# Attention outputs brought into channel order by DMA instead of by transposes on TensorE

## Chip, cores and metric

The kernel runs on one core of a Trainium2 chip. The metric is the device time of one execution in microseconds (us), and the lower the better. A measurement of this kernel can tell a difference of about 0.2% from none.

## What is computed

A layer on x of shape (8, 1024, 256), float32: layer norm, then attention and a gated feed-forward part side by side, both added to x. The part that the change touches is the end of attention:

```python
q, k, v = heads(xn @ Wq + bq), heads(xn @ Wk + bk), heads(xn @ Wv + bv)   # 16 heads of 16
q, k = rotary(q), rotary(k)
att = (einsum('bhid,bhjd->bhij', q, k) + bias) / sqrt(16)                 # causal, T = 1024
att = softmax(where(causal, att, -inf))
y = einsum('bhij,bhjd->bhid', att, v)
y = y.transpose(0, 2, 1, 3).reshape(B, T, C)                              # channels: head * 16 + d
attention = y @ Wp + bp
```

The feed-forward part (16 columns of 64 neurons, of which a gate chooses one column for each token, with a layer norm behind it) is computed in the same loop and fills TensorE between the pieces of attention.

## The kernel before

The program is written by hand, engine by engine. One list of stages (function `iteration`) is walked by every engine, and each engine issues its own instructions of a stage; semaphores join them. So the order of the list is the order on every engine, the DMA queue of SyncE (SP) included. SP issues nearly all DMAs, one after another, and it waits in that order too.

The loop runs over 8 batches and in each over 4 groups of 4 heads: 32 iterations, called b0 g0 to b7 g3 below. An iteration holds 40 slots. A slot is one tile of transposed scores (keys on partitions, up to 512 queries in columns): TensorE multiplies (L1158), VectorE adds the near-diagonal bias where there is one (L1341, L1343, L1345), ScalarE takes the exponential (L1037) into `probs`. Every fourth slot TensorE multiplies `probs` by the values (`pv`, L1175) into `o_bank`, one PSUM bank: head h of the group stands in partitions 32h to 32h+15 as 16 values by 512 queries, and partition 32h+16 holds the softmax sum, since `v_aug` has a column of ones. The queries come in two halves. ScalarE copies `o_bank` to `o_sb` (stage `o_out`, L1045): half 0 after the pv of slot 16, half 1 in the closing part of the iteration.

Beside the slots stand, by the table `BESIDE`, the projection of a later chunk of x (`qk`, `v`), the rotary turn (GpSimd and VectorE), the split of q and k into three bf16 parts, the gate, the feed-forward part (`neurons` L1259, `columns` L1270), and `row` tiles: TensorE computes the next group's scores the other way round (L1196) and VectorE takes their maxima (L1365, L1370), from which comes the shift of the softmax. `with_rows` places these 40 tiles of an iteration by weights for TensorE and VectorE (`PE_TIME`, `DVE_TIME`).

At the end of an iteration (`CLOSING`): `load` (12 DMAs) and `load_v` fetch a later group's operands; `shift` reduces the maxima on VectorE; `shift_turn` transposes them on TensorE (L1243), ScalarE copies them (L1086), SP writes them by 3 DMAs into rows of `stack_q` (L812), and the first score of the next iteration waits for those DMAs. Between `shift_turn` and that score TensorE has the first 12 matmuls of `columns` (`OPENING`). VectorE's `center` (L1419) writes the normalized x of a later chunk.

How an output half gets to the result: `o_turn`, slot 21 for half 0, and just ahead of `shift_turn` for half 1: TensorE transposes `o_sb` in 4 pieces into one of the two PSUM banks of the pair (L1277); VectorE takes reciprocals of the sums (L1397) and multiplies (L1400) into `y`, with queries on partitions. In the last group of a batch and in g0 of the next, for each 256 tokens (chunks 0, 1 in g3; chunks 2, 3 in g0): `y_turn` transposes `y` back in 4 pieces (L1282, slots 26 and 32), ScalarE copies to `y_t` (L1100), and `project_begun`, `project` multiply by the output weights (L1288), VectorE adds the rest (L1533), SP stores (L827). The stages of `BANKED` take the two banks of the pair in turn, and the next user of a bank waits until the one before has been drained.

```python
elif stage == "o_turn":                                    # VectorE
    dve.wait_ge(bank_filled[i], use + 1)
    dve.reciprocal(inv[:, :, :], o4[:, :, :, D]).then_inc(inv_ready, 1)
    dve.wait_ge(inv_ready, k + 2)
    dve.tensor_tensor(dst..., o4[:, :, :, 0:D], inv..., ALU.mult).then_inc(bank_drained[i], 1)
```

## Time and profile before

| | |
|---|---|
| median of 3 runs | 1983.5 us (1981.84 to 1984.29) |
| the profiled execution | 1982.37 us |
| its span, first to last instruction | 1980.5 us |
| TensorE / VectorE / ScalarE / GpSimd busy | 91% / 82% / 56% / 32% |
| mean granted clock of TensorE | 0.978 of full |
| DMA | 189.44 MB, 96 GB/s on average |

PE is TensorE's matmul side, PEld its weight load, DVE is VectorE, ACT ScalarE, POOL GpSimd, SPq the DMA issues of SyncE. Times of rows are us from the start of the span. The chain is the sequence of work that ended last, followed back from the last instruction, so what lies on it costs time. The kernel is very regular: the transposes of half 0 come every 56.78 us in plain groups.

### The profile page before, as it was taken

What the parts mean: (1) busy time and instruction counts of PE and PEld (TensorE: products, weight loads), DVE (VectorE), ACT (ScalarE), POOL (GpSimd) and SP (SyncE); (2) the same over time, 40 slices, a digit from 0 to 9 for tenths busy, and PEclk for the clock granted to TensorE, in tenths of its full rate; (3) what the DMA queues carried; (4) which work ended last, traced back from release to release, by engine and by line L of the source; (5) the groups of instructions that cost most, each with busy time, mean ns of one, the idle gap of its engine ahead of it and who ended that gap; (6) DMA issues with size and microseconds to landing.
All of it is one profiled execution on the core that took longest, in us unless ns stands there. A gap on an engine that the chain in (4) does not pass through costs nothing.

```text
span 1980.5 us, 34962 instructions
## 1 busy us (share of the span) xinstructions
PE 1808.5 (91%) x10870; PEld 1041.2 (53%) x10870; DVE 1623.9 (82%) x5566; ACT 1112.3 (56%) x2150; POOL 629.2 (32%) x890
## 2 busy tenths in 40 slices
PE   5789999999999999999999999999999999999887
PEld 3555555554555555555555555565555555544433
DVE  5668988888888888888888888888888888878783
ACT  3326655556665566665555666555666555655544
POOL 6442333233333233233323333322323332311010
PEclk8789999999999999999999999999999999999998
DMA  6673223333233323422333332332333232232201
GB/s 188 191 163 97 78 88 99 104 94 96 91 92 100 113 68 97 123 88 86 98 96 90 112 92 76 103 109 78 102 97 105 84 100 83 65 87 70 59 12 49
DMA packets 220469, 189.44 MB, mean 96 GB/s; under 512 B 63387, under 2 KB 195371, under 8 KB 220284
## 3 DMA queue, kind: packets, MB, share of 16 engines
q1 hardware_dynamic: 219840, 186.83, 32.5%
q8 instruction: 87, 1.43, 0.3%
q14 instruction: 98, 0.80, 0.1%
q10 hardware_dynamic: 444, 0.38, 0.1%
HBM read 118.64 MB, written 69.27 MB: 95 GB/s over the span
## 4 chain that ended last, share of the span: by engine, by line
PE 52%; DVE 31%; ACT 7%; issue 6%; DMA 2%; SPq 1%; ACTq 0%; DVEq 0%; POOL 0%; POOLq 0%
PE rows L1196 10%; PE o_bank L1175 9%; PE scores L1259 9%; PE scores L1158 7%; DVE rows L1365 6%; DVE scores L1343 5%; DVE maxima L1370 5%; PE bank L1270 5%; PE bank L1288 3%; ACT probs L1037 3%; PE bank L1220 3%; PE scores L1261 2%; DVE maxima L1365 2%; PE bank L1214 2%; DVE scores L1345 1%
## 5 line engine op out<-in xcount | busy, mean ns | idle before, releaser
L1037 ACT ACTIVATE probs<-scores 128x512 f32<-128x512 f32 (+1 forms) x1280 | 672.0, 555 | 518.3 <-DVE scores L1343 302.9
L1370 DVE TENSOR_REDUCE maxima<-rows 128x1 f32<-128x512 f32 (+4 forms) x896 | 479.8, 552 | 167.2 <-PE rows L1196 163.5
L1158 PE MATMUL scores<-stack_q,stack_k 99*128 99x512 bf16 (+3 forms) x1536 | 431.8, 332 | 78.0 <-ACT probs L1037 70.0
L1196 PE MATMUL rows<-stack_k,stack_q 96*128 96x256 bf16 (+3 forms) x2048 | 460.9, 291 | 15.8 <-DVE maxima L1365 7.1
L1365 DVE CUSTOM_DVE_ANT_0 rows<-rows,near_rows 128x256 f32<-128x256 f32 (+1 forms) x1024 | 394.2, 431 | 48.0 <-PE rows L1196 47.4
L1196 PEld LDWEIGHTS rows<-stack_k,stack_q 96*128 96x128 bf16 x2048 | 175.2, 98 | 316.1 <-issue 114.4
L1343 DVE TENSOR_TENSOR scores<-scores,near_cols 128x256 f32<-128x256 f32 x768 | 321.1, 431 | 17.0 <-PE scores L1158 16.8
L1175 PE MATMUL o_bank<-probs,v_aug 128*32 128x512 f32 (+3 forms) x3072 | 317.1, 500 | 2.8 <-ACT probs L1037 2.8
L1259 PE MATMUL scores<-again,w_cols 128*128 128x256 f32 x1024 | 274.7, 391 | 3.1 <-DMA b_cols<-in_b_cols_dram 3.1
L1270 PE MATMUL bank<-w_proj,act_t 128*128 128x256 f32 x1024 | 255.4, 382 | 22.7 <-DVE y L1400 22.3
L1158 PEld LDWEIGHTS scores<-stack_q,stack_k 99*128 99x128 bf16 x1536 | 140.3, 98 | 250.1 <-ACT probs L1037 194.6
L1094 ACT ACTIVATE act_t<-scores,b_cols 128x256 f32<-128x256 f32 x256 | 107.5, 471 | 206.1 <-PE scores L1261 205.9
L1270 PEld LDWEIGHTS bank<-w_proj,act_t 128*128 128x128 f32 x1024 | 185.6, 189 | 53.5 <-DVE y L1400 30.7
L1259 PEld LDWEIGHTS scores<-again,w_cols 128*128 128x128 f32 x1024 | 183.7, 194 | 27.8 <-DMA b_cols<-in_b_cols_dram 3.2
L957 POOL TENSOR_TENSOR part<-qk,part 128x512 bf16<-128x512 f32 x64 | 74.1, 1158 | 271.3 <-ACT part L1078 271.2
L1365 DVE DVE_READ_ACCUMULATOR2_ANT maxima<- 128x1 f32 x1024 | 144.4, 141 | 0.1
L1220 PE MATMUL bank<-kept,w_qkv 128*128 128x256 f32 x496 | 134.6, 404 | 3.0 <-ACT kept L1050 3.0
L975 POOL TENSOR_SCALAR norm<-moments 128x2 f32<-128x2 f32 x32 | 7.3, 227 | 369.4 <-issue 369.0
L881 POOL TENSOR_SCALAR norm<-moments 128x2 f32<-128x2 f32 x32 | 7.2, 224 | 368.3 <-issue 362.2
L1175 PEld LDWEIGHTS o_bank<-probs,v_aug 128*32 128x32 f32 x3072 | 67.3, 108 | 91.4 <-issue 74.4
L1220 PEld LDWEIGHTS bank<-kept,w_qkv 128*128 128x128 f32 x496 | 95.0, 201 | 20.4 <-issue 7.1
L891 POOL TENSOR_TENSOR y2n<-y2n,gain 128x256 f32<-128x256 f32 x64 | 45.4, 731 | 141.4 <-DVE y2n L1526 141.4
(123 smaller groups left out, 2107.3 us busy)
## 6 DMA issues: line engine op xcount, KB each, us to landing
parts_d<-part SPq DMA_DIRECT2D x96, 256.0 KB, 2.2
stack_q<-parts_d SPq DMA_DIRECT2D x378, 64.0 KB, 3.0
stack_k<-parts_d SPq DMA_DIRECT2D x378, 64.0 KB, 2.3
kept_d<-kept SPq DMA_DIRECT2D x31, 512.0 KB, 2.9
again<-kept_d SPq DMA_DIRECT2D x31, 512.0 KB, 3.3
x<-in_x_dram SPq DMA_DIRECT2D x32, 256.0 KB, 3.4
turns<-turns_d SPq DMA_DIRECT2D x32, 256.0 KB, 2.9
v_d<-v SPq DMA_DIRECT2D x32, 256.0 KB, 2.4
```

Source lines behind the costliest of these rows:

```text
L957: pool.tensor_tensor(parts[2][:, KC * t:KC * t + KC, :], qk[:, t], parts[1][:, KC * t:KC * t + KC, :], ALU.subtract).then_inc(lo_ready, 1)
L1037: act.activation(probs[:, (g * NS + s) % PROBS, h, 0:width], ring[(rings + ring_n[1]) % RING][:, 0:width], ACT.Exp, scale=float(D) ** -0.5 ...
L1094: ins = act.activation(act_t[:, mm, :], ring[(rings + ring_n[1]) % RING][:, m * CH:(m + 1) * CH], ACT.Gelu, bias=b_cols[:, mm:mm + 1])
L1158: ins = pe.matmul(ring[(rings + ring_n[1]) % RING][:, c0:c0 + w], stack_k[g % 2][:, h, kb * P:(kb + 1) * P], stack_q[g % 2][:, h, q0:q0 + ...
L1175: ins = pe.matmul(o_bank[32 * h:32 * h + 32, HALF - w:HALF], v_aug[g % 2][:, kb, h, :], probs[:, (g * NS + s) % PROBS, h, c0:c0 + w], star ...
L1196: ins = pe.matmul(tile[:, c0:c0 + k1 - k0], stack_q[ag % 2][0:STACK, h, qb * P:(qb + 1) * P], stack_k[ag % 2][0:STACK, h, k0:k1], start=Tr ...
L1220: ins = pe.matmul(bank[:, half * CH:(half + 1) * CH], w_qkv[:, k, cols:cols + P], normed(g)[1][:, k, :], start=(k == 0), stop=(k == KC - 1))
L1259: pe.matmul(dst, w_cols[:, k, mm * P:(mm + 1) * P], ffn_t[:, k, :], start=(k == 0), stop=False)
L1270: ins = pe.matmul(bank[:, t * C:(t + 1) * C], act_t[:, m, t * P:(t + 1) * P], w_proj[:, m, :], start=(m == 0), stop=(m == EM - 1))
L1343: dve.tensor_tensor(tile[:, 0:2 * P], tile[:, 0:2 * P], near, ALU.add))
L1365: ins = dve.tensor_tensor_reduce(tile[:, c0:c0 + w], tile[:, c0:c0 + w], near_rows[:, ag * GH + h, 2 * P - w:2 * P], 1.0, LOWEST, ALU.add, ...
L1370: ins = dve.tensor_reduce(maxima[:, part, m:m + n], tile[:, c0:c0 + n * w].rearrange("p (n w) -> p n w", w=w), AX.X, ALU.max)
```

## The change

- The transposes of `o_sb` and of `y` on TensorE go, with their banks, VectorE's multiply and ScalarE's copy to `y_t`. `y_t` now holds 256 channels (2 times 128 partitions) by 1024 tokens.
- `o_move` (slot 17 for half 0; behind `o_out` 1 in the closing part): SP issues 4 DMAs that spread each head's row of sums over 32 partitions of 16 values (`sums`), and 4 that move each head's 16 rows of 512 into their channels of `y_t`.
- `o_recip` on VectorE (slot 22; half 1 in slot 2 of the next iteration), 128 by 16 from SBUF. `o_store` (23; 3): SP writes the reciprocals to DRAM. `o_fetch` (25; 6): SP waits for that DMA and reads them back, each head's row repeated over 16 partitions, into `inv_b` (64 partitions by 512).
- `o_scale` (28; 10) on GpSimd, in every second group: one multiply of 128 by 512, float32, in place in `y_t`, for two groups at once.
- `project_begun` waits for `o_scale`. Chunks 0 and 1 are projected in g3 from slots 30 and 34 (28 and 35 before), chunks 2 and 3 in g0 from slots 22 and 26.
- In g2, `load` and `load_v` go to the very end of the closing part. After the last group the chain `o_recip`, `o_store`, `o_fetch`, `o_scale` runs by itself ahead of the last two projections.
- `gate_th` and `ranked` share the memory of other small tiles.

```diff
-          21: [('gate', None), ('o_turn', 0)],
-          23: [('cast', 0)],
-          25: [('left', 0), ('middle', 0)],
-          26: [('y_turn', 0)],
-          28: [('load_k', None), ('project_begun', 0)],
+          17: [('hidden', None), ('o_move', 0)],
+          22: [('o_recip', 0)],
+          23: [('o_store', 0), ('cast', 0)],
+          25: [('left', 0), ('o_fetch', 0), ('middle', 0)],
+          26: [('rest_back', 0)],
+          28: [('load_k', None), ('o_scale', 0)],
+          30: [('cast', 1), ('project_begun', 0)],
+          31: [('left', 1), ('project', 0)],
+          34: [('middle', 1), ('project_begun', 1)],
+          36: [('project', 1)]}
+EARLIER = {22: [("project_begun", 2)], 23: [("project", 2)], 26: [("project_begun", 3)], 28: [("project", 3)]}
+for _at, _stage in ((2, "o_recip"), (3, "o_store"), (6, "o_fetch"), (10, "o_scale")):
+    BESIDE[_at] = BESIDE[_at] + [(_stage, 1)]
...
-CLOSING = [("load", None), ("load_v", None), ("neurons", (0, 0)), ("neurons", (0, 1)), ("pv", NS - 1), ("o_out", 1),
+CLOSING = [("load", None), ("load_v", None), ("neurons", (0, 0)), ("neurons", (0, 1)), ("pv", NS - 1), ("o_out", 1), ("o_move", 1),
...
-           ("neurons", (3, 1)), ("tie", None), ("o_turn", 1), ("shift_turn", None), ("center", None)]
+           ("neurons", (3, 1)), ("tie", None), ("shift_turn", None), ("center", None)]
...
+        late = [("load", None), ("load_v", None)] if g == NC - 2 else []
+        plan += [stage for stage in CLOSING if stage not in late] + late
...
+                    elif stage == "o_move":
+                        k, rows, dst = value_half(b, g, arg)
+                        sp.wait_ge(o_out, k + 2)
+                        wait(sp, inv_ready, k)
+                        for h in range(GH):
+                            sp.dma_start(sums[32 * h:32 * h + 32, :],
+                                         o_sb[32 * h + D:32 * h + D + 1, :].rearrange("o (n e) -> o n e", e=D)) \
+                                .then_inc(sums_in, 16)
+                        for h in range(GH):
+                            sp.dma_start(dst[h * D:(h + 1) * D], o_sb[32 * h:32 * h + D, :]).then_inc(y_in, 16)
+                    elif stage == "o_store":
+                        sp.wait_ge(inv_ready, k + 1)
+                        wait(sp, inv_in, k * 16)
+                        sp.dma_start(inv_d[k % 2].rearrange("h (n e) -> (h n) e", e=D), inv[:, :]).then_inc(inv_out, 16)
+                    elif stage == "o_fetch":
+                        sp.wait_ge(inv_out, (k + 1) * 16)
+                        wait(sp, y_ready, b * NG + (g // 2 * 2 + arg - 1))
+                        sp.dma_start(inv_b[rows, arg, :], bass.AP(inv_d.tensor, (k % 2) * GH * HALF,
+                                                             [[HALF, GH], [0, D], [1, HALF]])).then_inc(inv_in, 16)
...
+                    elif stage == "o_scale":
+                        if g % 2 == 0:
+                            continue
+                        pool.wait_ge(inv_in, (k + 1) * 16)
+                        pool.wait_ge(y_in, (k + 1) * GH * 16)
+                        dst = y_t[:, g % NG // 2, arg * HALF:(arg + 1) * HALF]
+                        pool.tensor_tensor(dst, dst, inv_b[:, arg, :], ALU.mult).then_inc(y_ready, 1)
...
-                        act.wait_ge(inv_ready, k + 1)
+                        wait(act, y_in, k * GH * 16)
+                        wait(act, sums_in, k * GH * 16)
                         act.activation(o_sb[:, :], o_bank[:, :], ACT.Copy).then_inc(o_out, 1)
...
                     elif stage in ("project_begun", "project"):
+                        pe.wait_ge(y_ready, projected(b, g) * NG + (NG - 1 + arg // 2))
```

## Rows read from the trace of the kernel before

**Rows 1.** The page, part 4: shares of the chain that ended last.

```profile
PE 52%; DVE 31%; ACT 7%; issue 6%; DMA 2%; SPq 1%; ACTq 0%; DVEq 0%; POOL 0%; POOLq 0%
```

**Rows 2.** Windows, slot 21 to shift, b0 g1, b0 g3: us, then busy PE, PEld, DVE, ACT, POOL.

```profile
232.52:260.48 27.96, 25.68 (x157) 11.76 (x155) 22.73 (x73) 17.61 (x37) 6.82 (x10) 1.00 0.32 90
...
346.03:377.16 31.13, 29.81 (x182) 16.01 (x180) 25.06 (x80) 18.26 (x39) 5.50 (x8) 1.00 0.43 120
```

**Rows 3.** Waits of TensorE, whole span: total us, times, longest.

```profile
PE bank L1270 <- DVE y L1400: 22.3, 30, 1.0
PE bank L1288 <- ACT y_t L1100: 11.5, 28, 0.8
PE scores L1158 <- DMA stack_q<-shift_t: 5.4, 8, 3.5
```

**Rows 4.** The chain in order of time, b3 g3: start us, us, what.

```profile
1047.31 0.48 PE bank L1277 x4
```

**Rows 5.** Timeline, end of b3 g2: start us, us, engine line, [idle before <- releaser].

```profile
1018.29 1.79 SPq L812 DMA_DIRECT2D stack_q<-shift_t  x3
1019.23 2.86 PE L1270 MATMUL bank<-w_proj,act_t 128*128 128x256 f32 x12 [0.97 <-DVE y L1400]
1021.92 0.38 PE L1158 MATMUL scores<-stack_q,stack_k 99*128 99x512 bf16 x1
1022.62 0.46 DVE L1343 TENSOR_TENSOR scores<-scores,near_cols 128x256 f32<-128x256 f32 x1
```

**Rows 6.** Timeline: load_v, shift ending b0 g1, b3 g3; shift, score ending b7 g2.

```profile
253.03 0.59 SPq L764 DMA_DIRECT2D v_in<-v_d  x1
260.22 1.79 SPq L812 DMA_DIRECT2D stack_q<-shift_t  x3
...
1073.55 0.59 SPq L764 DMA_DIRECT2D v_in<-v_d  x1
1078.56 1.79 SPq L812 DMA_DIRECT2D stack_q<-shift_t  x3
...
1930.29 1.77 SPq L812 DMA_DIRECT2D stack_q<-shift_t  x3
1933.48 1.44 PE L1158 MATMUL scores<-stack_q,stack_k 99*128 99x512 bf16 x3 [3.53 <-DMA stack_q<-shift_t]
```

**Rows 7.** One line each (durations ns min/median/max), and DMA issues (last: us to landing).

```profile
L812 SPq DMA_DIRECT2D stack_q<-shift_t x96: 508/591/1133, 147.0 to 1931.5; - x96
L702 SPq DMA_DIRECT2D stack_k<-parts_d x378: 302/426/1611, 66.9 to 1874.5; - x189
...
L1419 DVE TENSOR_SCALAR kept<-x,moments,rstd x62: 404/911/1431, 33.5 to 1664.3; 128x256 f32<-128x256 f32 x62
...
parts_d<-part SPq DMA_DIRECT2D x96, 256.0 KB, 2.2
...
v_in<-v_d SPq DMA_DIRECT2D x32, 256.0 KB, 3.1
...
stack_q<-shift_t SPq DMA_DIRECT2D x96, 8.0 KB, 1.8
```

**Rows 8.** Timeline, b3 g3: GpSimd's 128x512, the reciprocal, pv of slots 28 and 32.

```profile
1046.79 1.27 POOL L940 TENSOR_TENSOR qk<-qk,turns 128x512 f32<-128x512 f32 x1
...
1047.98 0.25 DVE L1397 RECIPROCAL inv<-bank 128x16 f32<-128x16 f32 x1
...
1051.44 1.07 PE L1175 MATMUL o_bank<-probs,v_aug 128*32 128x512 f32 x8
...
1056.66 1.07 PE L1175 MATMUL o_bank<-probs,v_aug 128*32 128x512 f32 x8
```

**Rows 9.** Timeline, the last 20 us: output copy and the last projections.

```profile
1965.12 0.60 ACT L1045 ACTIVATE o_sb<-o_bank 128x512 f32<-128x512 f32 x1 [0.98 <-PE o_bank L1175]
...
1968.85 3.43 PE L1288 MATMUL bank<-w_out,y_t 128*128 128x256 f32 x8 [0.84 <-ACT y_t L1100]
...
1973.55 1.97 PE L1288 MATMUL bank<-w_out,y_t 128*128 128x256 f32 x8 [0.84 <-ACT y_t L1100]
```

More of the change, by code:

```diff
@@ L208 @@
 NEEDS = {"qk_begun": "x_turn", "qk": "x_turn", "v": "x_turn", "hidden": "x_turn",
-         "project_begun": "y_turn", "project": "y_turn",
-         "y_turn": "o_turn", "y2_stats": "columns"}
+         "y2_stats": "columns"}
 class Order:
@@ L256, in iteration, with behind, here @@
                     plan.append(("o_out", 0))
-            plan += [(stage, arg + 2 * (g == 0) if stage in ("y_turn", "project_begun", "project") else arg)
-                     for stage, arg in BESIDE.get(i, [])]
+            plan += BESIDE.get(i, []) + EARLIER.get(i, [])
         plan += [("pv", s) for s in range((SLOTS - 1 - PV_AFTER) // GH + 1, NS - 1)]
-        plan += CLOSING
-        def here(stage):
-            return (has_front if stage in FRONT
+        late = [("load", None), ("load_v", None)] if g == NC - 2 else []
+        plan += [stage for stage in CLOSING if stage not in late] + late
+        def behind(stage, arg):
+            return stage in ("o_recip", "o_store", "o_fetch", "o_scale") and arg == 1
+        def here(stage, arg):
+            return (batch + g > 0 if behind(stage, arg)
+                    else g == NG - 1 if stage == "rest_back"
+                    else has_front if stage in FRONT
                     else batch + (g + LEAD + 1) // NC < B if stage in FRONT_AHEAD
@@ L268, in here @@
                     else has_load if stage in ("load_q", "load_k", "load", "load_v")
-                    else (g == NG - 1 or (g == 0 and batch > 0)) if stage in ("y_turn", "project_begun", "project")
+                    else (g == NG - 1 if arg < 2 else g == 0 and batch > 0) if stage in ("project_begun", "project")
                     else True)
-        plan = [(stage, arg) for stage, arg in plan if here(stage)]
+        plan = [(stage, arg) for stage, arg in plan if here(stage, arg)]
         if has_next:
@@ L274, in iteration @@
         for stage, arg in plan:
-            o.add(stage, g + (stage in FRONT_AHEAD) - (stage in FRONT_BEHIND), arg)
+            o.add(stage, g + (stage in FRONT_AHEAD) - (stage in FRONT_BEHIND) - behind(stage, arg), arg)
     if batch == B - 1:
+        for stage in ("o_recip", "o_store", "o_fetch", "o_scale"):
+            o.add(stage, NG - 1, 1)
         for k in range(NC // 2, NC):
-            o.add("y_turn", NG - 1, k)
             o.add("project_begun", NG - 1, k)
@@ L561, in ffn_of, with value_half @@
             return fb, c, fb * NC + c
+        def value_half(b, g, half):
+            rows = slice((g % 2) * GH * D, (g % 2 + 1) * GH * D)
+            return b * (2 * NG) + (2 * g + half), rows, y_t[rows, g % NG // 2, half * HALF:(half + 1) * HALF]
         def next_group(b, g):
@@ L1482, in body @@
                         step(5)
[L1483 removed]
+                        dve.tensor_reduce(first[:, :], tied[:, :, :], AX.X, ALU.max).then_inc(chosen, 1)
                         step(6)
[L1485 removed]
+                        dve.tensor_tensor(others[:, :, :], tied[:, :, :], each(first[:, :]), ALU.not_equal) \
                             .then_inc(chosen, 1)
```

85 lines of the change are left out of this document (30 added, 55 removed).

## The prediction

> **What bounds the kernel now.** I read the chain first: half of it is TensorE and a third VectorE [rows 1]. So neither engine's busy time can be taken as the time, and the next question is which of them holds which stretch. The chain in order of time repeats one pattern in every iteration. From `center` to about slot 15 it runs mainly over VectorE (row maxima, bias adds), from there to the shift mainly over TensorE, where a transpose of half 0 is on it with 0.48 us for four pieces [rows 4]. The windows show how tight TensorE is in the second part: busy 25.68 of 27.96 us in a plain group and 29.81 of 31.13 us in a group with two projections [rows 2]. From these two I take the rate at which TensorE work turns into time there: 3.17 us of span for 4.13 us of work, 0.77. The rest is hidden in waits on ScalarE and VectorE that become shorter.
>
> The waits say what the turns cost besides their own time: 22.3 us at the first `columns` matmul, which needs the bank that half 1's multiply has just drained, and 11.5 us in 28 waits of the projections for ScalarE's copy [rows 3].
>
> **Part by part.** The sum is made against the profiled execution, 1982.4 us (span 1980.5 and 1.9 around it), which is 1.1 below the median of the runs.
>
> *Half 0's turn goes.* TensorE loses 0.48 us [rows 4] in 31 iterations; the last is treated below. VectorE loses its multiply, while the reciprocal (0.25 us [rows 8]) stays, from SBUF. At 0.77 the 0.48 us are 0.37, times 31: -11.5 us. If TensorE counted in full, -14.9; if VectorE and ScalarE hid it all, 0.
>
> *The turns back go.* 28 of the 32 lie inside the loop ahead of the last group: 0.48 us for the same four pieces and 11.5 / 28 = 0.41 us of waiting [rows 3, 4]. At 0.77: 28 x 0.89 x 0.77 = -19.2 us; in full -24.9.
>
> *A new wait ahead of the projections in g3.* In g0 the operands of chunks 2 and 3 are scaled from slot 10 on, well ahead of slot 22. In g3 there are 8 slots between `o_recip` and `project_begun`. I place the chain in b3 g3. The reciprocal ends at 1048.2 [rows 8]. The store to DRAM: nearest row 2.2 us to landing [rows 7], so 1050.5. The fetch from DRAM, 128 KB: between 1.8 (the smallest row) and 3.1 (256 KB in pieces of 256 bytes) [rows 7]; I take 3.1, since a read behind a write had the longer rows, so 1053.6. GpSimd's 128 x 512 takes 1.27 us [rows 8]: about 1055.0 with its signals. TensorE gets there earlier than before. From the pv of slot 28 (1051.44) to that of slot 32 (1056.66) are 5.22 us [rows 8], of which 1.97 are a projection at full clock [rows 9] and 0.41 its wait; 2.8 us are left for four slots, so slot 30 comes 1.9 us behind 1051.44, and 0.96 us earlier for the two turns that are gone: 1052.4. TensorE stands still for 2.6 us, and queued behind it are the scores and rows that feed ScalarE and VectorE. Seven times 2.6 x 0.77: +14.0 us. The bounds: 1.3 us a time with a fetch of 1.8, +7; 5 us a time if both DMAs land over a microsecond later, +27.
>
> A rule of the Trainium skill speaks against this fetch: "DMA: Bandwidth & Descriptors", section "Why a DMA increments its semaphore by 16 and not by 1", says that a DMA is spread over the largest number of engines up to 16 that divides the slowest dimension of both sides. The fetch's source begins with a dimension of 4 heads, so 4 engines would carry it. No row here shows such a shape at this size. Were its landing 1 us longer by that, the stall would be 3.6 us and the forecast about 5 us higher.
>
> *The end of the iteration.* Here 0.48 us of turn and 0.74 us of wait (22.3 / 30) [rows 3, 4] leave TensorE, but something else is late next. `columns` could start 1.4 us ahead of 1019.23, and the score behind it can't follow: it needs the shift DMAs. These are issued from 1018.29 [rows 5], when ScalarE has come to its copy behind the last gelu, which the turn doesn't delay. Where only the DMAs hold the score it starts 3.19 us after the first issue (1930.29 to 1933.48) [rows 6]; that gives 1021.48 here instead of 1021.92 [rows 5]. VectorE is better off: without its reciprocal and multiply `center` starts some 0.6 us earlier, the row maxima follow, and the first bias add needs the score: 1021.48 + 0.38 + 0.07 = 1021.93 instead of 1022.62 [rows 5]. That is 0.69 us at the start of a stretch that VectorE holds, less 0.25 us for `o_recip` of half 1 in slot 2: 0.44 us. Eight iterations waited for the DMAs before [rows 3] and get nothing; 23 x 0.44 = -10.1 us. From above, all of 1.22 us counted 31 times: -38.
>
> This rests on SP. Between `load_v` and the shift DMAs it now has 8 issues and a wait for an output copy that is long done. An issue took 0.43 us (16 rows) or 0.59 us (the shift's) as a median [rows 7], so 3.4 to 4.7 us; the gap was 6.6 us in b0 g1 (253.62 to 260.22) and 4.4 us in b3 g3 [rows 6]. I take 0.5 us, 4.0 in all: hidden. If they don't fit, the excess is paid one for one. In g2 the loads are out of the way. They then start near 1020 in b3 and end their issue 6 to 7 us later; the late rows that need them come more than 12 us behind the shift, so I cost them at nothing. If that cover were gone, a microsecond would be paid 7 times. `o_store` and `o_fetch` of half 1 hold SP for some 2.5 us at slots 3 to 6, ahead of the DMAs of slot 7, which wait for ScalarE anyway.
>
> *The last group and the tail.* Nothing runs beside this chain at the end. `o_sb` is complete at 1965.72 [rows 9]. Four issues of 0.5 us, the last started 1.5 us in and landed after 1.8: 1969.1. Reciprocal 0.25; SP is through with 8 issues at 1969.8; store 2.2, fetch 3.1, multiply 1.27: 1976.4. The projection began at 1968.85 [rows 9], so +7.5 us. It ran at half clock then (3.43 against 1.97 us for 8), after TensorE had mostly waited; I assume the same again. Inside the last group the same stall of some 3 us is met by a stretch in which TensorE waits anyway, less the turns: +1.6. Together +9.1 us, between +5 and +14.
>
> **The sum.** -11.5 - 19.2 + 14.0 - 10.1 + 9.1 = -17.7 us. 1982.4 - 17.7 = 1964.7 in the profiled execution's terms, 1966 us as a median.
>
> **The rivals.** *B: TensorE is the bound and its time counts in full.* For it: busy 92% and more in the second half [rows 2]. Against it: the factor 0.77 and the shift DMAs. -14.9 - 24.9 - 38 + 7 + 9 = -62: 1922 us. Half way is as likely as the end, so I read this case as 1915 to 1952. Chance 0.22.
>
> *C: SP's queue takes the place of the turn, slower than before.* The 8 issues of half 1 stand straight ahead of the shift DMAs. It decides from 4.4 / 8 = 0.55 us per issue in g3 and 6.6 / 8 = 0.82 us in g1. The shift's own issues reached 1.13 us and the loads' 1.61 [rows 7], and a row of 64-byte pieces isn't in the trace. At 1.1 us they take 8.8 us: the first score is 2.2 us late after a gap of 6.6 and 4.4 us after one of 4.4. With about 16 and 7 such iterations +66 us; at 0.9 us, 16 x 0.6 + 7 x 2.8 = +29, and the 10.1 are lost: 1966 + 39 = 2005. Range 1985 to 2040, chance 0.15.
>
> *D: the new waits are near the upper bounds.* Stalls of 5 us in g3 (+27 in place of 14) and nothing at the iteration's end: 1966 + 13 + 10 = 1989; with one of the two, 1976 to 1979. Chance 0.12, and this is most of the case of no difference.
>
> *E: GpSimd's multiply holds up VectorE.* `center`'s instructions took 404 ns at least and 911 as a median, up to 1431 [rows 7], where they run beside GpSimd's work on `y2n`. There are 32 new multiplies of 1.27 us, next to maxima and bias adds. If each held VectorE for its length in half of the cases: 16 x 1.27 = +20, 1986 us. The 0.46 us bias adds show nothing of the kind. Chance 0.03. The Trainium skill, "SBUF — State Buffer", section "SBUF: two separate sides", says that the two engines share a port pair, locked for a whole instruction; by that rule an operation with one SBUF input and the other in PSUM isn't held, which keeps E small.
>
> **How the numbers follow.** The forecast A has 0.48, from 1953 to 1979 by the bounds of its terms. The range must reach into B below and into C and D above: 1935 to 1992 leaves out about half of B and most of C. Faster by over 0.2% (under 1979.5; 0.2% is about what a measurement tells from no change): A nearly whole, B, a third of D: 0.73. Within 0.2%: 0.08. Slower: C, half of D and E: 0.19.
>
> **What would show it.** The score that opens an iteration starts 3.2 us behind the first shift issue, and TensorE has an idle piece there that the shift DMAs end. The shift's issue follows ScalarE's copy without SP being late (C otherwise). The projections in g3 wait for GpSimd by 1 to 4 us, those in g0 don't. Plain groups get 0.8 us shorter (56.0 instead of 56.8), g0 some 2 us, g3 hardly at all. The tail from `o_sb` to the projection is near 10.5 us instead of 3. If plain groups shorten by over 1.5 us, B was right; if they lengthen, C.

## The result, and the profile after

The changed kernel takes 1999.55 us (median of six runs, 1993.13 to 2002.82) beside 1984.54 us of the kernel before in the same series: 1.0076 times, with a 95% interval of 1.0061 to 1.0092. It is slower by 15 us, where I had forecast 18 us faster (1966, range 1935 to 1992). The profiled execution has a span of 2001.0 us against 1980.5.

The page of the kernel after, parts 1 and 4; part 4 answers to [rows 1]. Its mean granted clock is 0.965 of full, where the kernel before had 0.978.

```profile
PE 1782.2 (89%) x10486; PEld 1001.3 (50%) x10486; DVE 1583.7 (79%) x5502; ACT 1093.3 (55%) x2086; POOL 670.2 (33%) x922
...
PE 49%; DVE 22%; ACT 8%; issue 6%; DMA 6%; SPq 4%; POOL 4%; ACTq 0%; POOLq 0%; DVEq 0%
```

GpSimd, SP's queue and the DMAs, together 3% of the chain before, hold 14% of it now. The waits of TensorE (total us, times, longest) answer to [rows 3]:

```profile
PE scores L1200 <- ACT probs L1085: 84.9, 145, 2.6
PE bank L1321 <- POOL y_t L992: 29.3, 9, 12.2
PE scores L1200 <- DMA stack_q<-shift_t: 20.1, 32, 5.5
PE bank L1312 <- ACT act_t L1143: 13.9, 31, 0.5
```

The two waits that the change was to take away, 22.3 and 11.5 us, are gone. In their place stand 29.3 us in nine waits for GpSimd's multiply (seven in g3 of b0 to b6, one in the last group, one in the tail), 14.7 us more for the shift DMAs and a new 13.9 for the gelu. The chain says the same: the kernel lost TensorE work and gained chains of small DMAs.

Where the time went, from one shift DMA to the next on SyncE's timeline (before and after; b0 g0 is the first iteration):

| stretch | before, us | after, us | difference | forecast |
|---|---|---|---|---|
| start to the first shift DMA | 147.0 | 148.5 | +1.5 | 0 |
| g0, g1 and g2 of b0 to b6 without b0 g0, 20 iterations | 1154.7 | 1140.3 | -14.5 | -23 |
| b0 g0 | 56.4 | 56.3 | -0.1 | -1 |
| g3 of b0 to b5, 6 iterations | 361.6 | 368.2 | +6.5 | 0 |
| b6 g3, b7 g0, g1, g2 (the work thins out) | 210.5 | 221.4 | +10.9 | -3 |
| last group and tail | 50.2 | 66.3 | +16.1 | +9 |
| sum | 1980.5 | 2001.0 | +20.5 | -18 |

The forecasts of the parts are my terms spread over the iterations that they were counted for. A plain group (g1 or g2) mostly took 56.78 us before; of the 14 in b0 to b6, 11 take 56.01 to 56.08 now, so the forecast of 56.0 holds. A g0 went from 59.90 us to between 58.4 and 58.6 (two at 59.2 and 59.4), where 57.7 was forecast. A g3, forecast level with before at 60.3, shows two kinds: 60.04, 60.27 and 60.28, or 62.23, 62.37 and 62.97.

The difference between the two kinds is seen in the timeline of b1 g3 of the kernel after, 584 to 592 us (start, duration, engine and line, idle time before and its releaser):

```profile
583.11 0.59 SPq L851 DMA_DIRECT2D inv_b<-inv_d  x1
587.20 1.26 POOL L992 TENSOR_TENSOR y_t<-y_t,inv_b 128x512 f32<-128x512 f32 x1 [1.21 <-DMA inv_b<-inv_d]
588.61 1.55 PE L1321 MATMUL bank<-w_out,y_t 128*128 128x256 f32 x4 [2.43 <-POOL y_t L992]
```

and in that of b0 g3, with the windows around it (us, busy PE, PEld, DVE, ACT, POOL, then the granted clock):

```profile
353.86 2.05 PE L1321 MATMUL bank<-w_out,y_t 128*128 128x256 f32 x4 [2.07 <-POOL y_t L992]
...
349.60:353.00 3.40, 2.19 (x13) 0.37 (x11) 2.49 (x7) 2.49 (x6) 2.13 (x3) 1.00 0.86 224
353.00:356.40 3.40, 2.54 (x7) 1.78 (x8) 0.03 (x1) 1.06 (x3) 0.71 (x1) 0.59 0.33 65
```

TensorE stood idle for 2.07 us, and behind that its clock was granted at 0.59 as a mean of the window, half level (1.2 GHz) for most of it: four projection matmuls took 2.05 us, which take 1.10 at the full level. VectorE did 0.03 us of work in 3.4 us, ScalarE a third of what it did before. In the kernel before nothing of the kind happens between 150 and 1736 us, and TensorE has no wait above 0.98 us there up to 1713. The first longer one stands in b6 g3, and the half level begins at 1736.3, right behind it:

```profile
1735.23 0.39 PE L1158 MATMUL scores<-stack_q,stack_k 99*128 99x512 bf16 x1 [1.83 <-ACT probs L1037]
```

In the kernel after, the half level begins at 353.6, 589.1, 1053.3 and 1408.3. The first three lie in g3, in exactly the three iterations of b0 to b5 that take 62 us or more. There the idle times were 2.07, 2.43 and 1.70 us; in those of 60.0 to 60.3 us they were 1.18, 1.04 and 1.18. The fourth lies in b5 g1, behind a wait of 1.21 us for ScalarE's probabilities, not for a projection.

The tail of the kernel after answers to [rows 9]:

```profile
1976.72 0.60 ACT L1094 ACTIVATE o_sb<-o_bank 128x512 f32<-128x512 f32 x1 [0.98 <-PE o_bank L1217]
1977.34 2.44 SPq L835 DMA_DIRECT2D sums<-o_sb  x4
1979.82 2.49 SPq L839 DMA_DIRECT2D y_t<-o_sb  x4
1980.93 0.25 DVE L1429 RECIPROCAL inv<-sums 128x16 f32<-128x16 f32 x1 [5.71 <-DMA sums<-o_sb]
1982.41 0.52 SPq L845 DMA_DIRECT2D inv_d<-inv  x1
1984.02 0.59 SPq L851 DMA_DIRECT2D inv_b<-inv_d  x1
1987.43 1.26 POOL L992 TENSOR_TENSOR y_t<-y_t,inv_b 128x512 f32<-128x512 f32 x1 [23.40 <-DMA inv_b<-inv_d]
1988.84 5.25 PE L1321 MATMUL bank<-w_out,y_t 128*128 128x256 f32 x16 [12.19 <-POOL y_t L992]
```

From `o_sb`'s end to the projection are 11.5 us where 3.13 stood before and 10.7 were forecast. Read it by its links: four issues of the sums 2.5, landing 1.1 behind the last, then the store could go at 1981.2 but SyncE is still issuing output moves until 1982.3; store 1.6, fetch 3.4, multiply 1.3, and 16 matmuls in 5.25 us at a mean granted clock of 0.70.

### The profile page after: what moved, and what is told of

It is laid out like the page before. It is cut to its first block, busy times and chain, and to the rows that moved or that the text cites. A ratio compares the mean times of both kernels' runs of the same rounds, so it can differ in the third digit from the quotient of the medians.

```text
span 2001.0 us, 34921 instructions
## 1 busy us (share of the span) xinstructions
PE 1782.2 (89%) x10486; PEld 1001.3 (50%) x10486; DVE 1583.7 (79%) x5502; ACT 1093.3 (55%) x2086; POOL 670.2 (33%) x922
## 4 chain that ended last, share of the span: by engine, by line
PE 49%; DVE 22%; ACT 8%; issue 6%; DMA 6%; SPq 4%; POOL 4%; ACTq 0%; POOLq 0%; DVEq 0%
PE scores L1301 11%; PE rows L1238 9%; PE o_bank L1217 8%; PE scores L1200 7%; DVE rows L1397 5%; DVE scores L1375 5%; PE bank L1312 4%; ACT probs L1085 4%; DVE maxima L1402 4%; DMA stack_q<-shift_t 3%; PE bank L1262 3%; PE scores L1303 3%; PE bank L1321 2%; SPq L827 2%; DVE maxima L1397 1%
## 5 line engine op out<-in xcount | busy, mean ns | idle before, releaser
L1200 PE MATMUL scores<-stack_q,stack_k 99*128 99x512 bf16 (+3 forms) x1536 | 437.9, 336 | 108.8 <-ACT probs L1085 84.9
L1312 PE MATMUL bank<-w_proj,act_t 128*128 128x256 f32 x1024 | 254.6, 381 | 13.9 <-ACT act_t L1143 13.9
L1005 POOL TENSOR_TENSOR part<-qk,part 128x512 bf16<-128x512 f32 x64 | 74.1, 1158 | 221.9 <-ACT part L1127 221.6
L1321 PE MATMUL bank<-w_out,y_t 128*128 128x256 f32 x256 | 74.0, 418 | 29.3 <-POOL y_t L992 29.3
```

What stands on the lines that cost most here:

```text
L1200: ins = pe.matmul(ring[(rings + ring_n[1]) % RING][:, c0:c0 + w], stack_k[g % 2][:, h, kb * P:(kb + 1) * P], stack_q[g % 2][:, h, q0:q0 + ...
L1312: ins = pe.matmul(bank[:, t * C:(t + 1) * C], act_t[:, m, t * P:(t + 1) * P], w_proj[:, m, :], start=(m == 0), stop=(m == EM - 1))
L1321: ins = pe.matmul(bank[:, t * C:(t + 1) * C], y_t[:, k, at:at + P], w_out[:, k, :], start=(k == 0), stop=(k == KC - 1))
```

## The experiments

All ratios are to the kernel before on the same chip in the same series. The theory from the two traces: the saved TensorE work is real, and what eats it is the idle time before the projection in g3, the fall of TensorE's clock that follows it, and the tail. The rivals: SyncE's queue, VectorE held by GpSimd's multiply, and the placing of the loads.

**Projections four to five slots later.**

```
-  30: [('cast', 1), ('project_begun', 0)],  31: [('left', 1), ('project', 0)],
-  34: [('middle', 1), ('project_begun', 1)],  36: [('project', 1)]
+  30: [('cast', 1)],  31: [('left', 1)],  34: [('middle', 1), ('project_begun', 0)],
+  35: [('project', 0)],  37: [('project_begun', 1)],  39: [('project', 1)]
```

> The changed kernel with only the projections of chunks 0 and 1 in g3 moved from slots 30/31 and 34/36 to 34/35 and 37/39. Theory S (the loss inside the loop is the stall of TensorE ahead of the first projection, 1.0 to 3.0 us in b0 to b6 and 4.5 us in the last group, and the stretches of half clock that follow it): the stalls vanish in b0 to b6, g3 takes 60.3 us or a little less in every batch instead of up to 62.97, and the whole goes from 1999.6 to about 1985 (7 x 1.8 x 0.77 = 10 for the stalls, 4 x 1.9 for the clock, less in part because the tail stays). Theory Q (SP's 10 DMAs more per half, or GpSimd's multiply beside VectorE, is what costs): the stall goes but the iterations keep their length, total within 3 us of 1999.6.

Measured: 1977.98 us, ratio 0.9977 (0.9958 to 0.9996), span 1973.5. The waits of TensorE:

```profile
PE scores L1202 <- ACT probs L1087: 88.8, 146, 2.2
...
PE bank L1323 <- POOL y_t L994: 14.0, 2, 12.4
```

Of the nine waits two are left, those of the last group and the tail. There is no half clock from 150 to 1713 us. Four slots turn the slower kernel into a slightly faster one: the wait was the cost, not the work that was added. The gain is 7 us more than expected, for the g3 are shorter than the 60.3 expected: of those of b0 to b5 three take 58.8 us, the others 60.2, 59.5 and 60.4. At the end of those three SyncE is late, by 0.7, 0.9 and 1.7 us: the shift is ready and its DMAs are not issued, which is rival C of the prediction. In b0 to b5 it shows only once the stall is gone. In b5 g3:

```profile
1524.65 0.27 ACT L1137 ACTIVATE shift_t<-bank 96x128 bf16<-96x128 bf16 x1
1526.61 1.85 SPq L829 DMA_DIRECT2D stack_q<-shift_t  x3
```

The issue comes 1.7 us behind the end of the copy, where it mostly is 0.02 to 0.03.

**TensorE kept at work in the wait.** Four matmuls of no use stand ahead of the wait of the first projection matmul (`arg` 0 in g3, `arg` 2 in g0). Each such float32 matmul stands as two in the trace.

```
+  if stage == "project_begun" and arg in (0, 2):
+      for _ in range(4):
+          pe.matmul(bank[:, 0:C], ident[:, :], w_out[:, 0, :], start=True, stop=True)
   pe.wait_ge(y_ready, ...)
```

> The changed kernel with four matmuls of 128x256 float32 (about 1.7 us of TensorE work whose result is overwritten) put ahead of the wait for GpSimd's multiply at the first projection of g3 and of g0. Theory S: what costs in g3 is the clock that falls behind the idle stretch more than the stretch itself. Then TensorE at work in place of waiting keeps full clock: no stretch at half clock in b0 to b5, g3 near 60.5 us in all of them (60.0 to 63.0 now), although work was added; g0 gets 1.3 us longer (7 x 1.3 = 9 us), so the total is about 1999.6 - 4 x 1.9 + 9 = 2001. If the clock falls for another reason, g3 keeps stretches of half clock and its 62 us in about four batches, and the total is 2008 or more.

Measured: 2001.14 us, ratio 1.0087 (1.0064 to 1.0109). The chain to the multiply is as long as before, so the projection starts no earlier; in b0 g3:

```profile
348.53 1.89 PE L1319 MATMUL bank<-w_out,ident 128*128 128x256 f32 x8
350.29 1.13 PE L1324 MATMUL bank<-w_out,y_t 128*128 128x256 f32 x4
...
346.00:350.00 4.00, 3.64 (x20) 1.90 (x21) 3.17 (x8) 3.06 (x7) 3.38 (x4) 1.00 0.83 213
350.00:354.00 4.00, 4.00 (x24) 2.11 (x23) 2.32 (x8) 1.53 (x3) 0.24 (x1) 1.00 0.28 48
```

The clock stays at the full level and the projection at 1.13 us. The g3 of b0 to b5 take 60.5 to 61.3 us, none 62 or more. What is won there is paid again in g0, where there was no wait to fill: 60.1 to 61.7 us in place of 58.4 to 59.4. The total is the 2001 that was expected, but it is made of a gain and a loss; the groups say more. In g3 the clock follows TensorE's idle time, and without its fall the three g3 of 62 us or more are 1.7 to 2.2 us shorter, though the wait is as long. One stretch at half level is left in b0 to b5, against the expectation: at 475.0 in b1 g1 (58.9 us), behind a wait of 1.69 us for ScalarE's probabilities, which these matmuls don't touch.

**The fetch in four DMAs.**

```
-  sp.dma_start(inv_b[rows, arg, :], bass.AP(inv_d.tensor, (k % 2) * GH * HALF, [[HALF, GH], [0, D], [1, HALF]]))
+  for h in range(GH):
+      sp.dma_start(inv_b[first_row:first_row + D, arg, :],
+                   bass.AP(inv_d.tensor, ((k % 2) * GH + h) * HALF, [[0, D], [1, HALF]]))
```

> The changed kernel, but each fetch of the inverse sums is four DMAs of 16 partitions in place of one DMA of 64. In the changed kernel GpSimd's multiply begins 4.0 us after the fetch's one issue in g3, where I had taken 3.1 from the landing of v_in. Theory F: the one DMA is slow in itself (its 64 rows go through few of the core's DMA engines); then each of the four lands faster, the fourth issue is only 1.8 us after the first, and from the first issue to the multiply it is again 4 us or a little less: the stalls before the projection in g3 stay at 1 to 3 us (mean 1.8), and the time stays within 3 us of the changed kernel's (ratio to the kernel before 1.006 to 1.009). Theory L: the landing is a fixed delay of the write and the semaphore, whatever the DMA's shape; then the fourth lands 4.0 us after its own issue, 5.8 after the first, the stalls grow by 1.8 us each, clock falls become more frequent, and the time is 12 to 20 us above the changed kernel's (ratio 1.014 to 1.018). In the tail F gives about the same 12.2 us of idle time, L gives 14. [...]

Measured: 1985.17 us, ratio 1.0013 (1.0001 to 1.0025); the profiled span is 1982.3. Both theories missed the total. The links in b1 g3, which answer to the rows of 583.11 to 588.61 above:

```profile
576.77 1.72 SPq L853 DMA_DIRECT2D inv_b<-inv_d  x4
579.95 1.26 POOL L995 TENSOR_TENSOR y_t<-y_t,inv_b 128x512 f32<-128x512 f32 x1 [0.39 <-DMA inv_b<-inv_d]
581.36 1.10 PE L1324 MATMUL bank<-w_out,y_t 128*128 128x256 f32 x4 [1.39 <-POOL y_t L995]
```

From the first issue to the multiply are 3.18 us here, 4.09 with one DMA. Wherever GpSimd waited for the fetch in g3 or g1, it was 3.1 to 3.4 us with four and 3.7 to 5.1 with one (3.4 only in the tail). The DMA table has 1.8 us from issue to landing for each of the four. So theory F was right that the one DMA is slow in itself, and too cautious in its size: splitting wins about 0.9 us although three issues come on top. The sentence of the Trainium skill weighed in the prediction ("DMA: Bandwidth & Descriptors", section "Why a DMA increments its semaphore by 16 and not by 1") fits these times: by it the one DMA, whose source begins with four heads, goes through 4 engines and each of the four, whose first dimension is 16, through 16. Which engines carried them isn't read from a row here.

The nine waits fell from 29.3 to 24.5 us in total, and that was worth 12 to 15 us. A part of the difference is the clock. In b0 g3 the stall fell from 2.07 to 1.19 us and the projection's four matmuls from 2.05 to 1.10:

```profile
349.21 1.10 PE L1324 MATMUL bank<-w_out,y_t 128*128 128x256 f32 x4 [1.19 <-POOL y_t L995]
```

All stalls of b0 to b5 lie at 0.87 to 1.50 us now, and behind none of them does the clock fall; the six g3 take 59.9 to 60.5 us. Of the 18.7 us between the two spans 3.8 lie ahead of the end of b0 g0, where the kernels hardly differ; that leaves 15. The medians differ by 14.4, and the ratios by 0.0063, which is 12.5 us. By stretches, the six g3 are 7.1 us shorter, for waits that are 2.7 us shorter; the last group and tail 0.9; and 5.5 lie in the light iterations, where a part may be chance, as is told below.

The waits are not shorter by 0.9 us each, for the fetch is not always the last link. In b0 to b5 GpSimd waited for it in three g3 of the kernel after (1.12, 1.21 and 0.47 us), and in one here (0.39). In the others the multiply stands right behind GpSimd's own split of q and k, which in the kernel after (L1005) had waited for ScalarE each time. In b5 g3 of that kernel:

```profile
1515.25 1.16 POOL L1005 TENSOR_TENSOR part<-qk,part 128x512 bf16<-128x512 f32 x1 [1.29 <-ACT part L1127]
1516.36 1.26 POOL L992 TENSOR_TENSOR y_t<-y_t,inv_b 128x512 f32<-128x512 f32 x1
```

There a quicker chain of DMAs brings nothing more; the multiply ahead of the split was not tried.

**GpSimd's multiply left out.** The division of the outputs by the softmax sums is not computed.

```
-  pool.tensor_tensor(dst, dst, inv_b[:, arg, :], ALU.mult).then_inc(y_ready, 1)
+  pool.sem_inc(y_ready, 1)
```

> The changed kernel with GpSimd's multiply left out (its waits stay, its semaphore is raised at once); left out of the computation is the division of the outputs by the softmax sums. Theory S (the multiply is one link of the chain to the projection, 1.27 us long, and no more): plain groups stay at 56.0 us, stalls before the projection in g3 fall from a mean of 1.8 us by 1.3 each, fewer of them pull the clock to half, g3 comes down from 61.5 to 59.5 or 60.0 us, tail and last group are 2 to 3 us shorter; in all 12 to 18 us below the changed kernel (1982 to 1988, ratio 0.999 to 1.002). Rival E (the multiply holds VectorE off the memory port while it runs): VectorE's chain in g3 and g1 would shorten too, by up to 1.3 us in each of the 16 groups with a multiply, g1 included, which would be seen in groups of 55 us and give 1975 or less.

Measured: 1975.46 us, ratio 0.9958 (0.9940 to 0.9976). Of the stalls in b0 to b5 one is left (0.73 us), their g3 take 58.8 to 59.9 us, and the plain groups stay at 56.00: VectorE isn't held by the multiply, neither in g1 nor anywhere. The gain, 24 us, is above the 12 to 18 expected; 13.6 of it lie in the six g3, where with the stalls gone the clock stays up too. It bounds what a quicker multiply can bring with the slots as they are.

**The loads of g2 back in their place.**

```
-  late = [("load", None), ("load_v", None)] if g == NC - 2 else []
+  late = []
```

> The changed kernel with one part of the change undone: in g2 the loads of q/k and v are issued at their old place at the head of the closing stages, not behind everything. Theory Q: the late loads in g2 make v_in land late in g3, where GpSimd waits for it ahead of its multiply and SP has 24 issues more behind it; with them in their old place the multiply in g3 begins 0.5 to 1 us earlier, the stalls fall to a mean near 1 us and the time by 5 to 10 us (1990 to 1995, ratio 1.003 to 1.005). Rival R: the stalls in g3 are the length of the chain recip - store - fetch - multiply alone; then they stay at a mean of 1.8 us, and the time stays within 2 us of the changed kernel's, or rises, where the 24 issues of 0.6 us now stand ahead of g2's output moves and hold o_sb, so that ScalarE's next copy and with it the output matmuls of g3 wait (up to +3 us each batch, 1999 to 2020).

Measured: 1998.48 us, ratio 1.0076 (1.0057 to 1.0096): the same time in another shape. The g2 take 56.0 to 57.0 us in place of 56.0, since the shift DMAs now queue behind 13 load issues and 8 moves (TensorE waits 25.1 us for them, 20.1 in the kernel after), and the g3 are shorter in three of six, longer in one (63.4, with a stall of 2.68 us). Theory Q is out. Rival R has the total (within 2 us) and nearly the mean of the seven stalls (1.65 us, expected 1.8), but not the new shape. The deferral is neutral here: it takes up to a microsecond out of g2 and puts it into g3.

**The output moves of half 1 behind the shift DMAs.** The four sums still go first.

```
-  for h in range(GH): sp.dma_start(dst[...], o_sb[...])     # in o_move, arg 1
+  ("shift_turn", None), ("o_rows", 1), ("center", None)]     # o_rows issues them
```

> The changed kernel with the 4 DMAs that move half 1's values put behind the 3 shift DMAs in SP's queue at the end of the iteration (the 4 for the sums stay ahead). Theory S: the queue reaches the shift in time in all but a few iterations (in 29 of 32 it waited for ScalarE), so nothing changes: 1999.6 within 2 us, perhaps 1 us less from b0 g3 and b2 g3 to g0. Theory Q (SP late at the shift): each iteration gets shorter by up to 1 us, total 1980 or less.

Measured: 2009.37 us, ratio 1.0138 (1.0106 to 1.0171). Both theories missed: neither had a loss of 10 us. The plain groups mostly stay at 56.02: SyncE wasn't late at their shift, so there was nothing to win. The one place where it was late in the kernel after is the shift that ends b7 g2, by 1.9 us:

```profile
1932.49 0.27 ACT L1135 ACTIVATE shift_t<-bank 96x128 bf16<-96x128 bf16 x1 [2.88 <-PE bank L1285]
1934.67 1.85 SPq L827 DMA_DIRECT2D stack_q<-shift_t  x3
```

Here that issue follows the copy at once, and b7 g2 takes 47.2 us in place of 49.1 (47.5 in the kernel before). The loss is in g3, 61.8 to 66.6 us. SyncE comes to the deferred loads of g2 later still, and GpSimd, whose queue is in order, waits for `v_in` with the multiply of the next group behind it (total, times, longest; 45.0 in 5 in the kernel after):

```profile
POOL v_aug L1020 <- DMA v_in<-v_d: 85.4, 7, 14.7
```

In b0 to b5 the multiply then waits for no DMA: it stands right behind the rest of GpSimd's queue and begins 0.7 to 3.8 us later than in the kernel after.

**One hop, and the reciprocal on the spread tile.** The sums go from `o_sb` to 16 partitions each at once, with no DRAM; VectorE inverts 128x512 in place of 128x16.

```
-  sums (4 DMAs), reciprocal 128x16, store inv_d, fetch inv_b
+  sp.dma_start(inv_b[first_row:first_row + D, arg, :], o_sb[32*h+D:32*h+D+1, :]...to_broadcast((1, D, HALF)))
+  dve.reciprocal(inv_b[:, arg, :], inv_b[:, arg, :])
```

> The changed kernel with the way of the sums shortened: no spread into 128x16, no store to DRAM and no fetch from it; 4 DMAs repeat each head's row of sums over 16 partitions straight from o_sb, and VectorE takes the reciprocal of 128x512 in place once for two groups (same slots), GpSimd multiplies as before. 8 issues of SP per half instead of 10. Theory S: GpSimd's multiply no longer waits for a round trip through DRAM; the operands are there some 5 us earlier, the stall in b0 to b6 is gone, the tail from the output copy to the projection takes 8.5 to 9.5 us instead of 11.5. VectorE gets 32 x 0.65 - 64 x 0.25 = +5 us of work. Total about 1999.6 - 18 - 2 + 3 = 1982. Theory Q: as GpSimd's work and 8 of 10 issues are the same, about 1996.

Measured: 2082.82 us, ratio 1.0505 (1.0481 to 1.0528). Both theories missed, by one number:

```profile
L1418 DVE RECIPROCAL inv_b<-inv_b 128x512 f32<-128x512 f32 x32 | 107.0, 3345 | 19.8 <-DMA inv_b<-o_sb 19.8
```

3.35 us for one reciprocal, against 0.24 for the 128x16 of the kernel after. Only the 32 halves with odd g are inverted, yet they cost 107 us of VectorE, ahead of bias adds and maxima that feed the other engines. In the loop the detour through DRAM is the cheaper of the two: it keeps the reciprocal at 16 elements per partition. In the tail, where VectorE has nothing else to do, the one hop is the shorter in spite of it: 10.1 us from `o_sb` to the projection in place of 11.5. A spread of the small reciprocals without DRAM was not tried.

**The tail alone.** The last half's moves are split between SyncE and ScalarE, and 24 matmuls of no use keep TensorE at work.

```
+  if batch == B - 1 and g == NG - 1: "o_move" 1 becomes "o_last" 1
+  o_last: SyncE issues sums 0, 1 and output 0; ScalarE sums 2, 3 and outputs 1, 2, 3
+  project_begun 2 of the tail: 24 x pe.matmul(bank[:, 0:C], ident[:, :], w_out[:, 0, :])
```

> The changed kernel, with the tail alone altered: the last half's eight moves are issued half by SyncE and half by ScalarE, and TensorE does 24 matmuls of no use (128x256) while it waits for the first projection of the tail. In the changed kernel o_sb's end to the first projection takes 11.5 us, of which 2.4 are the issues of the sums, 0.6 to 1.2 the y issues that hold the store, and the 16 matmuls behind it take 5.25 us at half the clock. Theory T (issues and clock are the tail's excess): the sums land 1.2 us earlier, the store goes 1.2 earlier still, o_sb to projection 9 us, the last projections at the full clock 2.5 us instead of 5.25: 4 to 6 us below the changed kernel (1993 to 1996), all of it behind the last group, loop unchanged. Rival: the chain is set by landings (2 + 1.5 + 4 us + 1.3), which the split does not touch; then less than 2 us is won.

Measured: 1994.34 us, ratio 1.0056 (1.0036 to 1.0077), 5 us less than the kernel after, as expected. Last group and tail take 61.9 us in place of 66.3:

```profile
1975.74 0.25 DVE L1454 RECIPROCAL inv<-sums 128x16 f32<-128x16 f32 x1 [4.72 <-DMA sums<-o_sb]
1976.02 0.35 SPq L857 DMA_DIRECT2D inv_d<-inv  x1
...
1982.84 3.62 PE L1346 MATMUL bank<-w_out,y_t 128*128 128x256 f32 x16
```

`o_sb` ended at 1973.12: 9.7 us to the projection in place of 11.5, and 3.62 us for 16 matmuls in place of 5.25.

**The mends together, and the last group.** Later projections, four fetches and the mended tail; then the same with the projections of chunks 0 and 1 of the last group moved into the tail's wait.

```
+  plan = [... for it in plan if not it[0].startswith("project")]          # last group only
+  project_begun 0, project 0, project_begun 1, o_recip, o_store, o_fetch, project 1, o_scale   # the tail
```

> The changed kernel with three mends together: g3's projections four to five slots later, each fetch as four DMAs of 16 partitions, and the tail's moves on two queues with 24 matmuls of no use in its wait. If the three costs are separate, as I hold (stalls with the clock that they lose; the tail's issues; the tail's clock), the gains add: the kernel with later projections alone took 0.9977 of the kernel before, the tail is worth 4 to 5 us, the fetch another 0 to 1 us (no stalls are left in the loop for it to shorten): ratio 0.994 to 0.996, the groups as with later projections alone (56.0, g3 58.8, g0 58.5), last group and tail 56 us in place of 61. Rival: where something common (VectorE's order, the loads' landing) sets the end of a batch, they do not add, and the ratio stays at 0.997 to 0.998.

> As the run with the three mends, but in the last group the projections of chunks 0 and 1 are taken out of the slots and put into the tail's wait, in place of a part of the matmuls of no use (20 stay). If the last group's lag of 7.2 us behind the kernel before is the wait of its half-0 projection for GpSimd (4.5 us) and the half clock behind it, the last group now loses neither, and 8 matmuls and two additions leave it: 3 to 5 us less than the run with three mends, ratio 0.992 to 0.994. Rival: the last group is set by ScalarE's and VectorE's work, and the projection's wait is hidden there; then it stays within 1 us of the other.

Measured: 1969.54 us, ratio 0.9933 (0.9916 to 0.9950), and 1968.83 us, ratio 0.9922 (0.9904 to 0.9940). Last group and tail take 57.3 and 56.1 us. The mends add up, a little better than the 0.994 to 0.996 expected, and the changed kernel so mended is faster than it was and than the kernel before. The step to the second kernel was expected to bring 3 to 5 us and brought 0.7, which can't be told from nothing; that is what its rival said. In it the matmuls of no use were too many: the multiply was done at 1960.53, TensorE at 1961.68.

```profile
1953.05 8.80 PE L1347 MATMUL bank<-w_out,ident 128*128 128x256 f32 x40
1959.26 1.27 POOL L1010 TENSOR_TENSOR y_t<-y_t,inv_b 128x512 f32<-128x512 f32 x1 [14.08 <-DMA inv_b<-inv_d]
1961.68 3.62 PE L1352 MATMUL bank<-w_out,y_t 128*128 128x256 f32 x16
```

## Why the prediction was wrong, step by step

The profiled execution changed by +20.5 us where -17.7 was forecast, 38 us apart. As an estimate from the rows below, some 10 us of them are the turns back, 7 the stalls in the seven g3, 7 the last group and the tail, 9 the rest of the light iterations, and the others are small, among them 1.8 us of half clock in b5 g1 and 1.5 ahead of the first shift. So no single term failed alone.

**Half 0's turn and the iteration's end: right.** Together -0.81 us for a plain group; measured -0.77 (56.78 to 56.01), within 0.06 us in 8 of the 14 groups g1 and g2 of b0 to b6; five of the others gained 0.2 to 0.65 us, and b5 g1 lost 0.95 to a fall of the clock. The route was as told. The end of b3 g2 in the kernel after, which answers to [rows 5]:

```profile
1016.50 1.79 SPq L827 DMA_DIRECT2D stack_q<-shift_t  x3
...
1019.69 0.38 PE L1200 MATMUL scores<-stack_q,stack_k 99*128 99x512 bf16 x1 [0.40 <-DMA stack_q<-shift_t]
1020.11 0.43 DVE L1375 TENSOR_TENSOR scores<-scores,near_cols 128x256 f32<-128x256 f32 x1 [0.44 <-PE scores L1200]
```

The score comes 3.19 us behind the first shift issue, as in [rows 6], and the shift DMAs end an idle piece of TensorE there in all 32 iterations. Rival C, SyncE late, did not decide, except at the end of b7 g2, where it took 1.9 us: its new issues took 0.59 us as a median, above my 0.5 and just above C's limit of 0.55 for g3, yet SyncE was waiting for ScalarE ahead of nearly all of the 32 (row of SyncE's waits: total, times, longest). It was close in b3 g3, where the last move ends at 1078.66 and the shift is issued at 1078.73. The stall itself had made the room, as the kernel with later projections shows.

```profile
SPq L827 <- ACT shift_t L1135: 58.8, 29, 6.5
...
1076.17 2.49 SPq L839 DMA_DIRECT2D y_t<-o_sb  x4
1078.73 1.82 SPq L827 DMA_DIRECT2D stack_q<-shift_t  x3
```

**The turns back: the size was half.** In size this is the largest of my terms that failed. I took 0.89 us at a rate of 0.77, so 0.69 for each and 1.37 for a group with two. Two kinds of group show it without a stall: g0 went from 59.90 to 58.45 and g3, in the kernel with later projections, from 60.28 to 58.83. Both are -1.45, of which 0.8 belongs to the plain group's part: 0.65 for two turns back, 0.33 each. The term is -9 us in place of -19.2. The rate of 0.77 came from adding whole projections with their additions; for the turns something else was next. TensorE's waits for ScalarE's probabilities rose from 70.0 us in 136 waits before to 84.9 in 145, which points to ScalarE; this was not tried apart.

**The stall in g3: placed too long, priced too low.** This is the step of the mechanism that failed. I had 2.6 us a time; measured are 1.04 to 2.99, mean 1.8. Slot 30 came later than I placed it: in b3 g3 TensorE stood ready 35.0 us behind the first shift issue and not 34.1. (My 1.9 us for two of four slots that take 2.8 doesn't follow either; half of it would have put the slot earlier still.) GpSimd's multiply ended there as placed, 36.5 us behind that issue and not 36.7, though with other links: the reciprocal stood a microsecond earlier, and the fetch took 3.8 us and not 3.1, in the other g3 that waited for it 4.0 to 5.1. With the rule of the Trainium skill ("DMA: Bandwidth & Descriptors", section "Why a DMA increments its semaphore by 16 and not by 1") applied I had written 3.6 us of stall; the longer landing was right and the larger stall wrong. The price was set at 0.77 of the length. Measured against the 58.83 of a g3 without a stall, 9.6 us of waits in b0 to b5 cost 15.2, a rate of 1.6: 1.2 to 1.45 us for stalls of 1.04 to 1.18, and 3.4 to 4.1 us for stalls of 1.70 to 2.43. So a short stall costs somewhat more than itself, for which no run shows the reason (SyncE isn't late at the end of these g3), and a longer one some 2 us more, because TensorE's clock is granted at half behind it. With about 6 us in b6 g3 (below) the term is some +21 us in place of +14.0. The clock was in my working for the tail alone. In the loop of the kernel before TensorE has no wait over 0.98 us up to b6 g3, so its trace shows full clock there, and I took that for a property of the loop rather than of its being busy; the row at 1735.23 was there to be read. The half clock at 1408.3 costs b5 g1 1.8 us.

**The light iterations: not costed.** b6 g3 to b7 g2 were forecast 3 us faster and came 10.9 slower. There the work thins out and the clock falls now and then in every kernel. The windows for b7 g0, before and after, and in the kernel with the mends:

```profile
1775.91:1830.26 54.35, 51.28 (x313) 28.06 (x313) 43.02 (x149) 29.05 (x58) 6.96 (x10) 0.97 0.25 70
```

```profile
1774.60:1832.35 57.75, 52.07 (x298) 26.69 (x298) 42.05 (x147) 28.02 (x54) 8.19 (x11) 0.91 0.29 75
```

```profile
1751.60:1805.59 53.99, 47.62 (x295) 24.93 (x293) 41.05 (x143) 26.86 (x54) 7.34 (x11) 1.00 0.31 81
```

PE is busy for 51.28, 52.07 and 47.62 us with clocks of 0.97, 0.91 and 1.00: the changed kernel has less work for TensorE and does it more slowly. Over the four iterations the time is 210.5 before, 221.4 after, 214.5 with later projections, 215.9 with four fetches, 211.0 and 215.4 with the mends. Two kernels that are alike up to the last group differ by 4.4 us here, so a part of the 10.9 is the chance of one execution; how much was not separated. Two parts can be named. Of the 6.9 us that later projections take away, 5.9 are in b6 g3, which has the seventh stall, of 2.99 us, and half clock behind it. And SyncE's late shift lengthens b7 g2, 49.1 us in place of 47.5.

**Last group and tail: +16.1 in place of +9.1.** The tail's chain was +8.4 (forecast +7.5): issues of 0.6 instead of 0.5, and the store waiting for SyncE's output moves, which I had seen and taken as 0.5 us. The group itself was +7.2 against +1.6. The stall there was 4.5 us, not 3, and stretches of half clock lie in it in both kernels, longer ones after. The last two kernels have 9 to 10 of the 16 us back.

**The rivals.** B (TensorE in full) is out: plain groups shortened by 0.77. E is out by the kernel without the multiply. D had the right sign and one right place, but its 1989 was made of stalls of 5 us, priced by their length, and of nothing gained at the iteration's end; neither came true, so its nearness is luck. None of the four had the clock in the loop. Its falls in three g3 and in b5 g1 cost some 8 us (an estimate: three times 2, and 1.8); without them the median would be at the upper edge of the range, and the forecast still 26 us off.

## What to carry to other kernels

Where TensorE sets the end and has as little idle time as here (91% busy before), price a new wait on its path twice: once by its length, and once by the clock that it may lose behind it. Here 1.2 us of idle time cost 1.4, and 2.1 us cost 3.5. So a chain of small DMAs that ends at such a wait is to be given slack in slots first (four slots were worth 1% of the kernel) and shortened second, with an eye on what its last engine has queued ahead of it; and a tail, where nothing hides it, pays every issue and landing in full. When work is taken from an engine, read what waits for the next engine rise before multiplying the saving by the count.

## What the runs showed of the hardware that was not expected

- VectorE's reciprocal of 128x512 takes 3345 ns and that of 128x16 244 ns, while an elementwise add of 128x512 took 0.69 us on it (L1560 of the kernel after). In a loop like this one the reciprocal belongs on the compact tile.
- The same 128 KB from DRAM to 64 partitions could be used 3.1 to 3.4 us after the first issue as four DMAs and mostly 4.1 to 4.4 us after it as one.
- TensorE's clock fell to half in the middle of a busy stretch. Idle times of 1.70, 2.07 and 2.43 us in g3 of the kernel after were followed by it, those of 0.87 to 1.50 us in it and in the kernel with four fetches were not. It isn't regular. In the kernel with the loads in their place 1.98 us was followed by a granted clock of 1.00, and 2.68 us by half level from 1051.4 to 1054.8. In the one with the tail alone mended the clock stayed at 1.00 behind 1.68 and 1.88 us, and in the one with the output moves behind the shift behind 2.76 us (b0 g3). And in b5 g1 of the kernel after it fell behind a wait of 1.21 us for ScalarE.
